# Four stacked conditional layers: the beginning of each scan run, with the copies of du's second half moved and the dt projection placed in two row tiles

## The chip, the cores and the metric

One core of a Trainium2 chip runs the whole program. The metric is the device time of one execution in microseconds; less is better. The engines run beside each other, each through a list of its own: PE is TensorE (matrix products and transposes; PEld is its weight load), ACT is ScalarE, DVE is VectorE, POOL is GpSimd, and SP issues the transfers. An engine executes its list in order and stops at a wait until another engine has counted a semaphore up.

## The reference, cut to what matters

Four layers follow each other on x of shape (2, 1024, 256). Layers 0 and 3 are attention-like. Layer 1 holds one selective scan, layer 2 holds two (one forward, one over the flipped sequence), each for both batch entries, so there are six scans over 1024 tokens, 512 channels and 16 states:

```python
xdbl = xm @ W_xp
dtr, Bm, Cm = jnp.split(xdbl, [DTR, DTR + DS], axis=-1)   # 64, 16, 16
dt = jax.nn.softplus(dtr @ W_dt + b_dt)
...
dA = jnp.exp(dt_t[:, :, None] * A)
hst = hst * dA + (dt_t * x_t)[:, :, None] * B_t[:, None, :]
y = jnp.einsum('bds,bs->bd', hst, C_t)
```

dtr has 64 columns, so the projection to dt contracts over 64 rows. "du" below is the product dt * x. All of it is in float32.

## The kernel before, in words

**A run.** One scan is a `Run` (q = 0 to 5). The 1024 tokens are two chunks of 512, taken in the order `r.order`. Channels lie on partitions in four blocks of 128 (`dt` 0 to 3 in the loops). A run has a beginning (`inputs_t`, `inputs_s`, `inputs_v` on PE, ACT, DVE) and a main part (`run_t`, `run_s`, `run_v`, `run_p`, `run_sp`).

**The beginning.** PE projects a chunk of the input to `xd` (`project_xd_t`, 96 rows: 64 for dt, 16 for B, 16 for C). ACT copies it from PSUM to `XD` in SBUF (`copy_xd_s`, L686). PE projects dt from rows 0 to 63 of it in four matmuls, one for each channel block (`project_dt_t`, L650). ACT takes Abs, Exp and Ln of dt (`size`, `decline`, `log`: L695, L699, L703), DVE the part max(dt, 0) (L763), the sum of the two (delta, L769) and du = delta * u (L771), in the buffer `DUD`. PE turns du of the first chunk into token-major form, four transposes into each of four banks (`turn_du_t`, L656), and ACT and DVE copy or scale the banks into SBUF (`copy_du_s` L735, `copy_du_v` L746, `scale_du_s` L731, `scale_du_v` L742). Between these steps the callbacks `more(0)` to `more(3)` do other work: in layer 1 the product of two weight matrices (`fuse_t`, before the first `turn_du_t`), in layer 2 the projections `z` (runs 2 and 4) or `gates` (runs 3 and 5), eight groups of four matmuls, of which three stand before the turn of du and four behind it. In layer 1 `meanwhile` is an addition and statistics on DVE, in run 2 an addition, in run 3 statistics.

**PSUM.** There are eight banks; `take` waits until the last user of the bank has been read (`banks.give`), and `seek` sets which bank comes next. The four dt banks of the second chunk are 3 to 6. The third group of `more(2)` takes bank 3, and the turned du takes 4 to 7, so both wait until DVE's L763 has read dt of the second chunk.

**The main part.** It has 128 units (16 states, 2 chunks, 4 channel blocks): unit i has a decay on ACT (`decay`, L930), an input formed on PE into banks 4 to 7 (`form_u`, four transposes L845 for even steps, four products L839 for odd ones, three units ahead of the scan) and a scan on DVE (L996). Two units make a pair: POOL multiplies it by C (L1015, 64 in a run), PE adds it up into banks 0 to 3 (`add_up`, L864; pair p at unit 2p + 7). ACT also scales du by B for later units (`scale_b` L907, `spread_b` L914) and keeps the last column of each pair of the first half (`keep`, L922), for which POOL waits. The scanned values have five slots, `r.H`; slots 1 to 4 lie on `DUD`. While the first units run, PE turns du of the second chunk into banks 0 to 3, one bank at each of units 0 to 3; ACT and DVE copy two each at units 3 and 4. `add_up` writes into the same banks, so pair 0 waits for these copies (`open_y`).

**SP.** `run_sp` fetches the rows of C for the steps (`c_load`, L800). In runs 1 and 5 SP first waits for the last turn of du's second chunk and then fetches the weights of the next layer (L1121, L1287), with the first row of C behind it in the same queue. Run 3 and run 5 are begun inside the run before them: `begin_two` projects and copies their first `xd` there.

Of the kernel before, what the change touches and what calls it, by code (L numbers as in the profile page):

```python
# [8 lines left out]
ALU = mybir.AluOpType  # L9
# [102 lines left out]
def program(nc, T, out):  # L112
    with ExitStack() as ctx:
# [495 lines left out]
        CAR = small[:, 136:200]  # L609
        XD = area(WK, S)  # L610
        A_B = [area(WK + 512 * j, 512) for j in range(4)]
# [34 lines left out]
        def project_dt_t(e, w, r, c):  # L646
            w.wait_ge(*act.at(("xd", r.q, c)))
            for m in range(4):
                o = take(w, ("dt", r.q, m, c))
                e.matmul(o, r.wdt[0:64, m * 128:(m + 1) * 128], XD[0:64, c * 512:(c + 1) * 512], start=True, stop=True).then_inc(*pe.up(("dt", r.q, m, c)))  # L650

# [32 lines left out]
        def copy_xd_s(e, w, r, c):  # L684
            w.wait_ge(*pe.at(("xd", r.q, c)))
            e.activation(XD[0:96, c * 512:(c + 1) * 512], bank(("xd", r.q, c))[0:96, :], ACT.Copy).then_inc(*act.up(("xd", r.q, c)))  # L686
            banks.give(("xd", r.q, c), act.now())

        def inputs_s(e, w, r, more, begun=False):
# [17 lines left out]
            more(0)  # L707
            e.preload_act_table_set("natural_log_exp_and_others")
            size(0)
            decline(0)  # L710
            copy_xd_s(e, w, r, r.order[1])
            more(1)
            size(1)
            for c in r.order:
                w.wait_ge(*pe.at(("bt", q, c)))
                e.activation(Bt[:, 4 * c:4 * c + 4, :], bank(("bt", q, c)).rearrange("p (j e) -> p j e", j=4)[:, :, 64:80], ACT.Copy).then_inc(*act.up(("bt", q, c)))
                banks.give(("bt", q, c), act.now())
            log(0)
            decline(1)
# [36 lines left out]
        def inputs_v(e, w, r, meanwhile=None, late=None):  # L756
            q = r.q
            for m in range(4):
                e.tensor_scalar(diag[:, m, :], ident[:, :], col(r.dcol, m), None, ALU.mult).then_inc(*dve.up(("diag", q)))
            for c in r.order:  # L760
                for m in range(4):
                    w.wait_ge(*act.at(("abs", q, m, c)))
                    e.tensor_scalar(r.DT[:, m, c * 512:(c + 1) * 512], bank(("dt", q, m, c)), col(r.bdt, m), 0.0, ALU.add, ALU.max).then_inc(*dve.up(("relu", q, c)))  # L763
                    banks.give(("dt", q, m, c), dve.now())
            for p, c in enumerate(r.order):
                o = slice(c * 512, (c + 1) * 512)
                w.wait_ge(*dve.at(("relu", q, c)))
                w.wait_ge(*act.at(("ln", q, p)))
                e.tensor_tensor(r.DT[:, :, o], r.DT[:, :, o], DUD[:, p, :, :], ALU.add).then_inc(*dve.up(("delta", q, p)))  # L769
                w.wait_ge(*dve.at(("delta", q, p)))  # L770
                e.tensor_tensor(DUD[:, p, :, :], r.DT[:, :, o], r.U[:, :, o], ALU.mult).then_inc(*dve.up(("du", q, p)))  # L771
                if meanwhile and p == 0:
                    meanwhile()
            if late:
                late()
            for j in range(4):
                if first_state(r, j)[2]:
                    scale_du_v(e, w, r, j)
            for j in range(4):
                if first_state(r, j)[2]:  # L780
                    copy_du_v(e, w, r, 0, j)
# [39 lines left out]
        def run_t(e, w, r, back=None, early=None):  # L821
# [54 lines left out]
            for i in range(UNITS):  # L876
                k, dt = divmod(i, 4)
                ci, s = r.steps[k]
                if dt % 2 and i >= 7:
                    add_up((i - 7) // 2)  # L880
                form_u(i + 3)
                if i < 4:
                    turn_du_t(e, w, r, 1, i)
                if dt == 3 and 4 <= s < 8:
                    add_skip(ci, s - 4)
# [10 lines left out]
        def run_s(e, w, r, y, more, early=None):  # L896
# [35 lines left out]

            w.wait_ge(*transfer(f"c_store{q}").at(0))
            w.wait_ge(*dve.at("neg_a"))
            for i in range(4):
# [4 lines left out]
            for j in range(4):  # L940
                if not first_state(r, j)[2]:
                    copy_du_s(e, w, r, 0, j)
            more(3)
            w.wait_ge(*act.at(("bt", q, r.order[1])))
            for j in range(4):
                spread_b(1, j)
            first_half(w, r)
            for i in range(UNITS):
# [5 lines left out]
                if i >= 4:  # L954
                    decay(i)
                if i in (3, 4):
                    copy_du_s(e, w, r, 1, i - 1)
                if dt % 2 and i >= 5:
# [13 lines left out]
        def run_v(e, w, r, y, back=None):  # L972
# [7 lines left out]
            for i in range(UNITS):  # L980
                k, dt = divmod(i, 4)
                ci, s = r.steps[k]
                if i == TAKEN_AT:
                    take_y(0)
                if i in (3, 4):
                    copy_du_v(e, w, r, 1, i - 3)
                w.wait_ge(*decayed.at((q, i)))
# [123 lines left out]
        def layer1_sp(e, w):  # L1111
# [7 lines left out]
            store_c_sp(e, w, runs[1])  # L1119
            w.wait_ge(*pe.at(("dut", 1, 1, 3)))  # L1120
            e.dma_start(W2[:, 0:2816], T["w2"][:, 0:2816]).then_inc(*transfer("w2").up(0))  # L1121
# [155 lines left out]
        def layer2_sp(e, w):  # L1277
# [3 lines left out]
            for q in range(2, 6):  # L1281
# [3 lines left out]
                if q == 5:  # L1285
                    w.wait_ge(*pe.at(("dut", 5, 1, 3)))
                    e.dma_start(W2[:, 0:2048], T["w3"]).then_inc(*transfer("w3").up(0))  # L1287
# [27 lines left out]
        def layer2_s(e, w):  # L1315
            for b in range(NB):
                one, two = runs[2 + 2 * b], runs[3 + 2 * b]

                def begin_two():
                    w.wait_ge(*scanned.at((one.q, UNITS - 2)))  # L1320
                    copy_xd_s(e, w, two, two.order[0])
# [649 lines left out]
```

## Time and profile before

| | |
|---|---|
| median of 3 runs | 1978.16 us (1977.44 to 1983.39) |
| the profiled execution's own time | 1980.28 us |
| span of its trace | 1978.5 us |
| granted TensorE clock, mean | 0.975 of full speed |
| busy: PE, DVE, ACT, POOL | 94%, 81%, 72%, 53% |
| POOL's multiplies L1015 | 384, 896.1 us |

The profile gives for each engine the time in which an instruction was in work; the share of the span is an average over stages that have different limits. In the six runs, some 1100 us of the span, four engines work nearly all the time, and what paces a stage has to be read from the rows of the stage. The last instruction of a chain is followed back to what released it; a share in that chain is not yet a bound where two engines are almost equally loaded.

### The profile page before, as it was taken

The page shows a single profiled execution, that of the slowest core. Times are in us where ns is not written, and L with a number is a line of the kernel's source. Part 1 is how long each engine was busy: PE and PEld are TensorE (multiplying, and loading weights), DVE is VectorE, ACT ScalarE, POOL GpSimd, SP SyncE. Part 2 cuts the span into 40 slices and gives each one's busy share as a digit, 9 for nine tenths or more (in the row PEclk, how much of TensorE's full clock was granted, in tenths as well). Part 3 has the DMA queues.
Part 4 walks back from the last instruction along what each step waited for, and adds up shares of the span by engine and source line. Part 5 has one row for each costly group of instructions (what it writes and reads, how often), then busy time and mean ns, then how long its engine had stood idle before and what let it go on. Part 6 is the DMA issues. An engine that isn't in the chain of part 4 may idle for free.

```text
span 1978.5 us, 32672 instructions
## 1 busy us (share of the span) xinstructions
PE 1865.9 (94%) x12312; PEld 1347.3 (68%) x12312; DVE 1605.2 (81%) x2125; ACT 1422.5 (72%) x2651; POOL 1049.9 (53%) x603
## 2 busy tenths in 40 slices
PE   6989899998999999989999999989998999999997
PEld 3664899748997499959995799679974333232323
DVE  5666899667997699889995999779987999999742
ACT  3426899368993799789974999779854277777775
POOL 3021699416994199929980599469953500003000
PEclk9989999998999999999999999989998799999999
DMA  5022211102111112102110111011101111111000
GB/s 198 1 97 84 65 57 57 49 12 73 57 57 49 34 55 60 49 18 60 55 43 2 38 58 57 23 63 57 55 24 28 41 40 37 37 36 37 19 23 22
DMA packets 57548, 95.19 MB, mean 48 GB/s; under 512 B 14951, under 2 KB 23559, under 8 KB 55982
## 3 DMA queue, kind: packets, MB, share of 16 engines
q1 hardware_dynamic: 55854, 88.90, 15.2%
q0 software_dynamic: 1536, 4.20, 0.7%
q8 instruction: 98, 1.61, 0.3%
q14 instruction: 60, 0.49, 0.1%
HBM read 73.55 MB, written 6.91 MB: 41 GB/s over the span
## 4 chain that ended last, share of the span: by engine, by line
PE 72%; POOL 9%; DVE 8%; issue 5%; ACT 4%; DMA 2%; SPq 1%; DVEq 0%; POOLq 0%; ACTq 0%
PE PS L839 12%; PE PS L864 12%; PE PS L256 9%; POOL A L1015 8%; PE PS L845 6%; PE PS L1599 6%; PE PS L1552 6%; PE PS L1759 5%; PE PS L265 3%; DVE A L1565 2%; PE PS L650 2%; PE PS L871 2%; PE PS L441 2%; PE PS L656 1%; PE PS L243 1%
## 5 line engine op out<-in xcount | busy, mean ns | idle before, releaser
L1015 POOL TENSOR_TENSOR A<-A 128x1024 f32<-128x1024 f32 x384 | 896.1, 2395 | 228.7 <-ACT small L922 163.1
L930 ACT ACTIVATE A<-A,negA 128x512 f32<-128x512 f32 x768 | 546.7, 714 | 32.1 <-DVE A L996 24.1
L996 DVE TENSOR_TENSOR_SCAN A<-A,PS 128x512 f32<-128x512 f32 x384 | 436.0, 1200 | 48.5 <-PE PS L845 19.6
L996 DVE TENSOR_TENSOR_SCAN A<-A,small,PS 128x512 f32<-128x512 f32 x384 | 453.6, 1257 | 8.5 <-ACT A L930 5.2
L864 PE MATMUL PS<-ident,A 128*128 128x128 f32 x3072 | 407.1, 276 | 15.2 <-POOL A L1015 11.8
L839 PE MATMUL PS<-A 128*128 128x128 f32 x3072 | 383.6, 276 | 3.6 <-ACT A L914 3.6
L864 PEld LDWEIGHTS PS<-ident,A 128*128 128x128 f32 x3072 | 353.9, 143 | 22.3 <-POOL A L1015 13.4
L839 PEld LDWEIGHTS PS<-A 128*128 128x128 f32 x3072 | 362.6, 192 | 5.8 <-DVE A L996 3.1
L1565 DVE TENSOR_REDUCE A<-PS 128x1 f32<-128x512 f32 x512 | 319.4, 681 | 40.8 <-PE PS L1552 39.4
L1796 ACT ACTIVATE A<-PS 128x512 f32<-128x512 f32 x512 | 267.5, 602 | 102.2 <-PE PS L1759 101.9
L907 ACT ACTIVATE A<-A,small 128x512 f32<-128x512 f32 x320 | 228.3, 713 | 21.5 <-PE PS L845 21.3
L845 PE MATMUL PS<-ident,A 128*128 128x128 f32 x1360 | 192.8, 280 | 20.5 <-ACT A L907 13.8
L1552 PE MATMUL PS<-A 99*128 99x512 bf16 x480 | 188.4, 401 | 13.0 <-DMA A<-scr 7.6
L1759 PE MATMUL PS<-A 102*128 102x512 bf16 x480 | 178.5, 385 | 5.1 <-ACT A L1796 4.9
L256 PE MATMUL PS<-A,W 128*128 128x512 f32 (+1 forms) x416 | 182.7, 594 | 0.5 <-ACT A L250 0.5
L845 PEld LDWEIGHTS PS<-ident,A 128*128 128x128 f32 x1360 | 160.9, 145 | 26.3 <-DVE A L996 20.2
L230 POOL TENSOR_TENSOR RS<-VE,HALF 128x8 f32<-128x8 f32 (+1 forms) x15 | 27.7, 1846 | 274.5 <-DVE VE L225 274.5
L1530 POOL CAST W<-W 128x32 bf16<-128x32 f32 x32 | 6.7, 211 | 291.8 <-DVE W L1523 217.4
L1552 PEld LDWEIGHTS PS<-A 99*128 99x128 bf16 x480 | 47.2, 98 | 167.3 <-DVE A L1565 122.1
L914 ACT ACTIVATE A<-ident,small 128x128 f32<-128x128 f32 x384 | 148.7, 393 | 6.2 <-PE PS L839 6.2
L256 PEld LDWEIGHTS PS<-A,W 128*128 128x128 f32 (+1 forms) x416 | 74.9, 184 | 97.8 <-issue 93.6
L1599 PE MATMUL PS<-A,W 128*32 128x512 f32 x1024 | 135.9, 604 | 0.0
(193 smaller groups left out, 1832.8 us busy)
## 6 DMA issues: line engine op xcount, KB each, us to landing
A<-scrc SPq DMA_DIRECT2D x192, 256.0 KB, 3.2
A<-A SPq DMA_DIRECT2D x360, 32.0 KB
scr<-A SPq DMA_DIRECT2D x4, 1024.0 KB, 4.8
W<-in_wa SPq DMA_DIRECT2D x2, 1536.0 KB, 9.8
X<-in_x SPq DMA_DIRECT2D x4, 512.0 KB, 5.5
scr<-W SPq DMA_DIRECT2D x128, 1.5 KB
out<-X SPq DMA_DIRECT2D x4, 512.0 KB, 3.0
W<-in_w SPq DMA_DIRECT2D x1, 1984.0 KB, 7.5
```

The source lines that it names most:

```text
L256: t = e.matmul(o[0:M, :], wt(k, m), act_in(k), start=k == 0, stop=k == nk - 1)
L839: t = e.matmul(o[:, j * 128:(j + 1) * 128], r.DUT[:, 4 * ci + j, dt * 128:(dt + 1) * 128], DB[k // 2 % 2][:, j, :], start=True, stop=True)
L845: t = e.transpose(o[:, j * 128:(j + 1) * 128], r.G[(2 * k + j) % 6][:, dt * 128:(dt + 1) * 128], ident[:, :])
L864: t = e.matmul(PS[:, j, dt * 128:(dt + 1) * 128], r.H[pair % HS][:, dt % 2, j * 128:(j + 1) * 128], ident[:, :], start=open_y(ci, j), stop ...
L930: e.activation(A_B[i % 4], r.DT[:, dt, ci * 512:(ci + 1) * 512], ACT.Exp, scale=negA[:, r.n, dt * 16 + s:dt * 16 + s + 1]).then_inc(*decay ...
L996: e.tensor_tensor_scan(h, a, u, init, ALU.mult, ALU.add).then_inc(*scanned.up((q, i)))
L1015: e.tensor_tensor(h, h, CB[k % 2].unsqueeze(1).broadcast_to([128, 2, 512]), ALU.mult).then_inc(*weighed.up((q, pair)))
L1552: e.matmul(o, SQ[j][0:99, nt * 128:(nt + 1) * 128], SK3[j][0:99, c * 512:(c + 1) * 512], start=True, stop=True).then_inc(*pe.up(("trial", ...
L1565: e.tensor_reduce(NM[:, k % 2, q:q + 1], bank(("trial", k, nt, c)), AX.X, ALU.max, negate=True).then_inc(*dve.up(("trial", k, nt, c)))
L1599: t = e.matmul(PV[32 * j:32 * j + 32, c, :], V[:, tile * 272 + 17 * h:tile * 272 + 17 * h + 32], PX[mt % 2][j][:, c * 512:(c + 1) * 512], ...
L1759: e.matmul(o, SK3[sl][0:102, mt * 128:(mt + 1) * 128], SQ[sl][0:102, c * 512:(c + 1) * 512], start=True, stop=True).then_inc(*pe.up(("scor ...
L1796: e.activation(PX[mt % 2][j][:, c * 512:(c + 1) * 512], bank(key), ACT.Exp).then_inc(*act.up(("weights", u, mt, j, c)))
```

## The change

The dt projection of channel blocks 1 and 3 reads rows 64 to 127 of the weights (they are stored twice) and of a second copy of xd, `XD2`, which ACT writes after the first; blocks 0 and 2 stay on rows 0 to 63. PE's wait for the projection is now for the second copy. ACT takes the logarithm of the first chunk before it goes on to the second chunk, and DVE does delta and du of the first chunk before the second chunk's L763; `meanwhile` comes ahead of delta. The turns of du's second chunk move from units 0 to 3 to units 1 to 4, ACT's copies of it from units 3 and 4 to 9 and 10, DVE's from 3 and 4 to 5 and 6, with a wait for the last turn ahead of scan 6. On ACT `more(3)` follows `spread_b(1, ...)`. Runs 3 and 5 no longer preload the table set. SP's two waits ahead of the weight loads are for earlier events.

```diff
-        XD = area(WK, S)
+        XD, XD2 = area(WK, S), area(WK + S, S)
...
         def project_dt_t(e, w, r, c):
-            w.wait_ge(*act.at(("xd", r.q, c)))
+            w.wait_ge(*act.at(("xd_twin", r.q, c)))
             for m in range(4):
-                o = take(w, ("dt", r.q, m, c))
-                e.matmul(o, r.wdt[0:64, m * 128:(m + 1) * 128], XD[0:64, c * 512:(c + 1) * 512], start=True, stop=True).then_inc(*pe.up(("dt", r.q, m, c)))
+                o, h, x = take(w, ("dt", r.q, m, c)), slice(m % 2 * 64, m % 2 * 64 + 64), XD2 if m % 2 else XD
+                e.matmul(o, r.wdt[h, m * 128:(m + 1) * 128], x[h, c * 512:(c + 1) * 512], start=True, stop=True).then_inc(*pe.up(("dt", r.q, m, c)))
...
         def copy_xd_s(e, w, r, c):
+            e.activation(XD2[64:128, c * 512:(c + 1) * 512], bank(("xd", r.q, c))[0:64, :], ACT.Copy).then_inc(*act.up(("xd_twin", r.q, c)))
...
-            e.preload_act_table_set("natural_log_exp_and_others")
+            if not begun:
+                e.preload_act_table_set("natural_log_exp_and_others")
             size(0)
             decline(0)
             copy_xd_s(e, w, r, r.order[1])
+            log(0)
             more(1)
             size(1)
...
-            log(0)
             decline(1)
             log(1)
...
-            for c in r.order:
+            for p, c in enumerate(r.order):
+                o = slice(c * 512, (c + 1) * 512)
                 for m in range(4):
                     w.wait_ge(*act.at(("abs", q, m, c)))
...
-            for p, c in enumerate(r.order):
-                o = slice(c * 512, (c + 1) * 512)
+                if meanwhile and p == 0:
+                    meanwhile()
                 w.wait_ge(*dve.at(("relu", q, c)))
                 w.wait_ge(*act.at(("ln", q, p)))
...
-                if meanwhile and p == 0:
-                    meanwhile()
...
-                if i < 4:
-                    turn_du_t(e, w, r, 1, i)
+                if 1 <= i < 5:
+                    turn_du_t(e, w, r, 1, i - 1)
...
+            w.wait_ge(*pe.at(("bt", q, r.order[1])))
...
-            more(3)
             w.wait_ge(*act.at(("bt", q, r.order[1])))
             for j in range(4):
                 spread_b(1, j)
+            more(3)
...
-                if i in (3, 4):
-                    copy_du_s(e, w, r, 1, i - 1)
+                if i in (9, 10):
+                    copy_du_s(e, w, r, 1, i - 7)
...
-                if i in (3, 4):
-                    copy_du_v(e, w, r, 1, i - 3)
+                if i in (5, 6):
+                    copy_du_v(e, w, r, 1, i - 5)
+                if i == 6:
+                    w.wait_ge(*pe.at(("dut", q, 1, 3)))
...
-            w.wait_ge(*pe.at(("dut", 1, 1, 3)))
+            w.wait_ge(*pe.at(("bt", 1, 1)))
             e.dma_start(W2[:, 0:2816], T["w2"][:, 0:2816]).then_inc(*transfer("w2").up(0))
...
-                    w.wait_ge(*pe.at(("dut", 5, 1, 3)))
+                    w.wait_ge(*pe.at(("mx", 1, 1, 1)))
                     e.dma_start(W2[:, 0:2048], T["w3"]).then_inc(*transfer("w3").up(0))
...
                 def begin_two():
-                    w.wait_ge(*scanned.at((one.q, UNITS - 2)))
+                    w.wait_ge(*scanned.at((one.q, UNITS - 1)))
```

## Rows read from the trace of the kernel before

**Rows 1.** The page: the chain that ended last, shares of the span

```profile
PE 72%; POOL 9%; DVE 8%; issue 5%; ACT 4%; DMA 2%; SPq 1%; DVEq 0%; POOLq 0%; ACTq 0%
```

**Rows 2.** Timeline of POOL in runs 1, 2, 5: start, us, instruction, idle before

```profile
461.53 27.93 POOL L1015 TENSOR_TENSOR A<-A 128x1024 f32<-128x1024 f32 x12 [15.17 <-DMA A<-scrc]
...
500.44 21.01 POOL L1015 TENSOR_TENSOR A<-A 128x1024 f32<-128x1024 f32 x9 [1.02 <-DVE A L996]
...
726.91 107.25 POOL L1015 TENSOR_TENSOR A<-A 128x1024 f32<-128x1024 f32 x46 [0.31 <-DVE A L996]
...
1305.66 37.32 POOL L1015 TENSOR_TENSOR A<-A 128x1024 f32<-128x1024 f32 x16 [45.94 <-DMA A<-scrc]
1344.08 16.44 POOL L1015 TENSOR_TENSOR A<-A 128x1024 f32<-128x1024 f32 x7 [1.09 <-DVE A L996]
```

**Rows 3.** Timeline of TensorE at the beginning of run 2

```profile
651.65 3.70 PE L650 MATMUL PS<-A,W 64*128 64x512 f32 x8
...
655.28 0.24 PEld L256 LDWEIGHTS PS<-A,W 128*96 128x96 f32 x2 [0.76 <-issue]
...
660.60 3.70 PE L650 MATMUL PS<-A,W 64*128 64x512 f32 x8
...
672.04 1.94 PE L656 MATMUL PS<-ident,A 128*128 128x128 f32 x16 [1.75 <-DVE A L771]
673.81 7.03 PE L256 MATMUL PS<-A,W 128*128 128x512 f32 x16
...
690.77 1.06 PE L845 MATMUL PS<-ident,A 128*128 128x128 f32 x8 [2.77 <-ACT A L907]
```

**Rows 4.** Timeline of ACT at the beginning of run 2

```profile
653.76 2.42 ACT L695 ACTIVATE A<-PS,COL 128x512 f32<-128x512 f32 x4
656.22 1.91 ACT L699 ACTIVATE A<-A 128x2048 f32<-128x2048 f32 x1
...
682.64 0.70 ACT L907 ACTIVATE A<-A,small 128x512 f32<-128x512 f32 x1
...
685.81 0.60 ACT L735 ACTIVATE A<-PS 128x512 f32<-128x512 f32 x1 [1.56 <-PE PS L656]
...
688.91 0.19 ACT L922 ACTIVATE small<-A 128x2 f32<-128x2 f32 x1
...
691.14 0.19 ACT L922 ACTIVATE small<-A 128x2 f32<-128x2 f32 x1
```

**Rows 5.** Timeline of SP in run 5: the weights of layer 3, then C

```profile
1298.98 0.33 SPq L1287 DMA_DIRECT2D W<-in_w  x1
1299.43 25.25 SPq L800 DMA_DIRECT2D A<-scrc  x6
```

**Rows 6.** Timeline of TensorE in runs 1 and 5: units 8 and 9 are formed

```profile
457.90 1.06 PE L845 MATMUL PS<-ident,A 128*128 128x128 f32 x8 [2.77 <-ACT A L907]
...
1302.61 1.74 PE L845 MATMUL PS<-ident,A 128*128 128x128 f32 x8 [2.77 <-ACT A L907]
```

**Rows 7.** Timeline of DVE at the beginning of run 2

```profile
662.48 3.33 DVE L763 TENSOR_SCALAR A<-PS,COL 128x512 f32<-128x512 f32 x4 [5.27 <-ACT A L695]
667.27 2.29 DVE L769 TENSOR_TENSOR A<-A 128x2048 f32<-128x2048 f32 x1 [1.46 <-ACT A L703]
```

**Rows 8.** Timeline of ACT at the beginning of run 3

```profile
842.22 1.28 ACT L708 ACT_TABLE_LOAD   x1 [0.23 <-DVE A L819]
...
873.49 0.73 ACT L907 ACTIVATE A<-A,small 128x512 f32<-128x512 f32 x1
```

**Rows 9.** Timeline of TensorE in run 0: the turn of du's first chunk

```profile
200.93 3.32 PE L656 MATMUL PS<-ident,A 128*128 128x128 f32 x16
```

**Rows 10.** Stretches of runs 1 and 2: us, PE, PEld, DVE, ACT, POOL busy, PEclk, DMA

```profile
461.00:465.00 4.00, 1.07 (x5) 1.07 (x6) 0.85 (x1) 2.82 (x6) 3.47 (x2) 0.50 0.02 7
465.00:469.00 4.00, 4.00 (x21) 4.00 (x20) 2.16 (x2) 1.36 (x4) 4.00 (x3) 0.50 0.30 69
...
692.00:696.00 4.00, 4.00 (x23) 4.00 (x23) 4.00 (x5) 4.00 (x11) 4.00 (x2) 0.59 0.21 44
```

More of the change, by code:

```diff
@@ L759, in inputs_v @@
                 e.tensor_scalar(diag[:, m, :], ident[:, :], col(r.dcol, m), None, ALU.mult).then_inc(*dve.up(("diag", q)))
-            for c in r.order:
+            for p, c in enumerate(r.order):
+                o = slice(c * 512, (c + 1) * 512)
                 for m in range(4):
                     w.wait_ge(*act.at(("abs", q, m, c)))
-                    e.tensor_scalar(r.DT[:, m, c * 512:(c + 1) * 512], bank(("dt", q, m, c)), col(r.bdt, m), 0.0, ALU.add, ALU.max).then_inc(*dve.up(("relu", q, c)))
+                    e.tensor_scalar(r.DT[:, m, o], bank(("dt", q, m, c)), col(r.bdt, m), 0.0, ALU.add, ALU.max).then_inc(*dve.up(("relu", q, c)))
                     banks.give(("dt", q, m, c), dve.now())
-            for p, c in enumerate(r.order):
-                o = slice(c * 512, (c + 1) * 512)
+                if meanwhile and p == 0:
+                    meanwhile()
                 w.wait_ge(*dve.at(("relu", q, c)))
```

## The prediction

> **What bounds the kernel now.** I read the page, then the timeline of POOL over the runs, then each engine's timeline over the beginnings. The chain gives most of the span to PE and little to POOL [rows 1], but in the runs this says little: in run 2 POOL does its last 46 multiplies in 107.25 us without a gap, 2.33 us each [rows 2]. It had a gap of 0.31 us before them; in runs 1 and 5, whose first multiply waited for the transfer of C, the gap at this place is 1.0 and 1.1 us [rows 2]. So from the 17th pair on POOL paces a run, and its end is the start of that pair plus 48 x 2.33 = 112 us. I call that start G: 500.4, 726.9 and 1344.1 us in runs 1, 2 and 5.
>
> What sets G? In run 2 PE waits 2.77 us for ACT before it forms unit 8 at 690.8, and from there it works through to G, 36.1 us later [rows 2, 3]; POOL's own first multiply needs ACT's `keep` at 688.9 [rows 4]. So where nothing else is late, G is PE's start of unit 8 (P) plus 36.1. In run 5 the first multiply comes at 1305.7 only, because C is behind the weights in SP's queue, issued at 1299.0 and 1299.4 [rows 2, 5]; run 1 has the same pattern (461.5, [rows 2]).
>
> The reader should therefore follow two things for each run: when P comes, and whether C is there.
>
> **SP's two waits.** In run 5 the multiply began 6.2 us after the issue of C [rows 2, 5]. P is 1302.6 [rows 6], so G without the late C would be 1338.8; it was 1344.1, which is 5.3 us. In run 1 P is 457.9 [rows 6], G would be 494.0 and was 500.4: 6.4 us. After the change run 1's weights are issued in the beginning, more than 5 us before u is ready, and run 5's when the last gates are projected, some 12 us earlier than now; C follows half a microsecond later and lands about when ACT keeps the first pair, which is before PE needs pair 0 (below). Gain 5.3 + 6.4 = 11.7 us. Run 0 has such a queue too, behind the second weight load of layer 1, which still waits for ACT's copies in `more(3)`; there C comes some 2 us after ACT is ready, but 1.5 us or more before PE can use the pair. It costs nothing as long as PE is held longer by the copies.
>
> **The beginning of runs 2 and 4.** I lay out run 2 anew, in times of the trace before.
> ACT: Exp of the first chunk ends at 658.1 [rows 4]. A copy of a bank takes 0.60 us, and the next may start after 0.5 [rows 4]; with xd's and its twin's, the twin is done at 659.2. The logarithm, as long as the Exp (1.9), ends at 661.0. It started at 665.3 before.
> DVE: delta and du take 2.3 us each [rows 7]: du is ready at 665.7, before at 671.9. Then come the four L763, some 0.7 us each while they need not wait (3.33 with waits, [rows 7]): 666.4, 667.1, 667.7, 668.4. The addition of 2.3 us fits between the first L763 and the logarithm; in layer 1's run 1 `meanwhile` is near 6 us and ends du 1.5 us later, but PE is busy with the weight product then.
> PE: the dt projection is eight matmuls at 0.43 us [rows 3]. A matmul of float32 is two such instructions on the same rows. In two row tiles the second of one block can run beside the first of the next, while the issue order is kept: five slots instead of eight, 2.2 us, 1.3 us saved. The trace has no two matmuls side by side; the bounds are 0 and the half, 1.8 us. I take 1.3. It ends the first projection at 653.9 and xd of the second chunk at 657.4; ACT is later than both. The second projection runs 659.3 to 661.5, B's turn until 662.2, two groups until 665.7; the third waits for L763 (666.4) and ends at 668.1. Du's four banks follow, 1.8 us, to 669.9. Before it was 673.8, so 3.9 us are won. `more(3)` takes 6.9 us [rows 3]: 676.8, before 680.7.
> ACT again: Abs until 664.1 (2.4 us for four, [rows 4]), B's copies, Exp, logarithm to 668.2; copies of three groups to 670.0; four decays, four copies (0.6 us from one start to the next) and four `spread_b` (half that, they are a quarter as wide) to 675.8; the four copies of `more(3)` end at 678.2. There unit 0 begins on ACT; before at 682.6 [rows 4]: 4.4 us.
>
> **The copies placed later.** ACT's loop needs 2.2 us for two units (`keep` to `keep`, 688.91 to 691.14, [rows 4]: three of 0.6, a `spread_b` of 0.3 and the 0.1 of `keep`). From its begin to P it took 8.1 us before, 1.6 of them waiting for a turn that ACT's copy needed; that wait and the two copies (1.0 us) leave the stretch, and the first `keep` comes at 682, so POOL starts 7 us earlier. But PE's `add_up(0)`, which stands before unit 10 is formed, waits for the copy that is now at unit 10: four units without decays 1.8, six units 6.7, one decay 0.6, two copies 1.0, together 10.1 us: 688.2. PE has formed 8 and 9 (0.9 us) and three of the eight transposes (0.3) by then, so this equals a P of 687.0, against 690.8: **3.8 us** in run 2, and as much in run 4, whose rows repeat it. The move of the copies by itself costs here what it wins; behind the held PE stand DVE's scan 10, which waits for the slot, and POOL, which has five pairs in hand and is starved only later, at G.
>
> Runs 3 and 5: the table load of 1.28 us [rows 8] goes, and it was on the path, since ACT could not start on dt. Exp ends at 846.6, du is ready at 854.2, the L763 end at 857.0, PE's turn of du at 858.6 (before 862.9), the gates at 865.4, ACT's unit 0 at 867.9 against 873.5 [rows 8]: 5.6 us, less 0.7 for the held `add_up` as in run 2, is **4.9** in each.
>
> Runs 0 and 1: du isn't awaited by PE, the weight product is. PE's path is twin copy +0.5, projections -2.6, one wait for ACT's Exp in place of one of 0.7 us: the turn of du starts at 198.7 instead of 200.9 [rows 9], 2.2 us. It ran at half speed (3.32 us for 16, run 2: 1.94, [rows 3, 9]), which may or may not recur; with ACT's copies behind it I take 2.9 us at unit 0, and after the 0.7 **2.2** in run 0, 2.5 in run 1.
>
> Sum: 2.2 + 2.5 + 3.8 + 4.9 + 3.8 + 4.7 (run 5, a little less, C being close) = 21.9, and 11.7 from SP: 33.6 us.
>
> **What the held PE costs in clock.** In run 1, where PE did 0.9 us of work from 457.9 and then waited until about 464 for POOL, the granted clock is 0.50, the lower level of 1.2 GHz, from 461 to 469 [rows 6, 10]: 5 us after PE resumed, half of them lost. In run 2, after 2.77 us of idle, it is 0.59 over the 4 us from 692 [rows 3, 10]: 3.3 us at the lower level, 1.6 lost. The new gap is 3 to 4 us of idle with 0.9 of work in it. I put it between: 1 us more in each run, bounds 0 and 2.5. That is 6 us. Forecast: 33.6 - 6 = 27.6 us off. The profiled execution had 1980.3 (span 1978.5 and 1.8 around it), 2.1 above the median; I take the gain from the median, 1978.2: 1950.6, so **1951**.
>
> The Trainium skill, "TensorE: Matmul & The Clock Gate", section "Part 3: Packing small matmuls", says that matmuls stay in strict order while those on different row groups run together, starting about 4 ns apart. With two instructions a block that is my five slots; no row here shows it.
>
> **The rivals.**
> (a) The clock doesn't fall further: 33.6 us, 1945. For: there is some work in the gap. Chance 0.15.
> (b) The row tiles don't overlap. Then PE, not ACT, paces the beginning: in run 2 the second projection ends at 664.2, `more(3)` at 678.8, gain 1.8; in runs 3 and 5 2.5; in runs 0 and 1 the twin's wait remains, -1.6. Sum 3.6 + 5.0 - 3.2 = 5.4, with SP's 11.7 about 17, less 6 for the clock: 11, 1967. For: rows on one tile show strict order. Chance 0.20.
> (c) Slower: each change between the two row tiles empties the array. Where the shape changes now, the weight load waits 0.76 us instead of 0.24 [rows 3], 0.5 us more. Three changes inside each of 12 projections are 1.6 us on each; with no overlap 3.1 us a run, nearly all on PE's path, some 19 us: 1967 + 19 = 1986. It decides from 0.3 us a change on. Chance 0.06.
> The skill's "TensorEngine Tiling (Array Packing)", section "Key Properties", speaks against (c): a change of mode drains, a change of tile does not. Half-height matmuls were in use before, so the mode is no new one.
> (d) POOL's own start counts, PE catches up: then each run gains what it gains at unit 0 (4.4, 5.6 and 2.9 us, two runs each, 25.8), the 2.6 of wait and copies (15.6) and, in runs 1 and 5, some 5 us of late C each, less 2 in run 0: 49 us, 1929. Against: PE has no gap between P and G. Chance 0.05.
> (e) It doesn't do what it says: the held `add_up` costs another 4 us a run (clock at half for two stretches, ACT late), and only SP's waits pay: within 5 us of before, 1973 to 1978. Chance 0.07.
>
> **How the numbers follow.** Forecast 0.47, the others as given. A difference under 0.3% (5.9 us) can't be told from none. Faster: forecast, (a), (b), (d) and a small part of (e), 0.88; same: most of (e), 0.06; slower: (c), 0.06. The range takes in (a) and (b) with 3 us at either side for the clock: 1940 to 1969; the likeliest case's own range is 1945 to 1956.
>
> **What the profile after would show.** The turn of du in run 2 (L656) starts some 4 us earlier after the previous run's end and follows L763, not du. L650's eight matmuls take 2.2 us; 3.7 is (b), over 5 is (c). Between forming unit 9 and `add_up(0)` PE idles 3 to 4 us on ACT's copy L735. POOL has a gap of 3 to 4 us in its first 16 multiplies or before the 17th; none is (d). In runs 1 and 5 no first multiply waits for a transfer by more than 1 us. No table load in runs 3 and 5. The forecast is wrong if PE's half-speed stretches last over 5 us in every run, or if PE isn't what G hangs on.

## The result and the profile after

The change makes the kernel faster: 1948.39 us (median of 4 runs, 1946.60 to 1949.29) against 1978.96 for the kernel before, run on the same chip (4 runs, 1977.44 to 1983.39). The ratio is 0.984, with a 95% interval of 0.982 to 0.986. The profiled execution took 1949.29 us, its span is 1947.4. The forecast was 1951, its likeliest case's range 1945 to 1956. In the round of the last four experiments one execution of the kernel before took 4806.18 us; it is part of no ratio.

G, POOL's 17th multiply, is where the prediction measures each run. It comes 30.4 us earlier in run 5, which is the whole gain. The page's chain has less of PE and more of ACT than [rows 1]:

```profile
PE 66%; POOL 9%; ACT 9%; DVE 8%; issue 6%; DMA 1%; SPq 1%; DVEq 0%; ACTq 0%; POOLq 0%
```

POOL's timeline of the kernel after, in runs 1, 2 and 5, against [rows 2]. The bracket is the idle time before the instruction and what ended it:

```profile
451.50 4.67 POOL L1019 TENSOR_TENSOR A<-A 128x1024 f32<-128x1024 f32 x2 [18.14 <-ACT small L923]
...
674.84 4.71 POOL L1019 TENSOR_TENSOR A<-A 128x1024 f32<-128x1024 f32 x2 [30.62 <-ACT small L923]
...
682.57 2.37 POOL L1019 TENSOR_TENSOR A<-A 128x1024 f32<-128x1024 f32 x1 [0.45 <-ACT small L923]
685.80 18.70 POOL L1019 TENSOR_TENSOR A<-A 128x1024 f32<-128x1024 f32 x8 [0.86 <-DVE A L1000]
705.44 9.51 POOL L1019 TENSOR_TENSOR A<-A 128x1024 f32<-128x1024 f32 x4 [0.95 <-DVE A L1000]
716.04 7.04 POOL L1019 TENSOR_TENSOR A<-A 128x1024 f32<-128x1024 f32 x3 [1.09 <-DVE A L1000]
...
1273.08 7.08 POOL L1019 TENSOR_TENSOR A<-A 128x1024 f32<-128x1024 f32 x3 [33.37 <-DMA A<-scrc]
```

Run 1's first multiply no longer waits for C. Run 2 begins its multiplies at 674.84, 14.4 us earlier than before (689.24), but needs 41.2 us to reach the 17th at 716.04, where sixteen multiplies without a gap take 37.3 (run 5, [rows 2]). Gaps of 0.22 to 1.09 us, the longer ones ended by DVE's scan, eat the nearly 4 us between.

PE and ACT of the kernel after at the beginning of run 2, against [rows 3, 4]:

```profile
644.59 2.83 PE L650 MATMUL PS<-A,W 64*128 64x512 f32 x8
...
652.67 1.99 PE L650 MATMUL PS<-A,W 64*128 64x512 f32 x8
...
661.46 1.91 PE L656 MATMUL PS<-ident,A 128*128 128x128 f32 x16
```

```profile
641.26 0.59 ACT L686 ACTIVATE A<-PS 96x512 f32<-96x512 f32 x1 [2.74 <-issue]
...
670.86 0.71 ACT L908 ACTIVATE A<-A,small 128x512 f32<-128x512 f32 x1
...
674.51 0.19 ACT L923 ACTIVATE small<-A 128x2 f32<-128x2 f32 x1
...
678.97 0.57 ACT L737 ACTIVATE A<-PS 128x512 f32<-128x512 f32 x1
...
680.53 0.58 ACT L737 ACTIVATE A<-PS 128x512 f32<-128x512 f32 x1
```

From ACT's first copy of xd to unit 0 (L908, L907 before) it is 29.6 us, before 34.3 (648.33 to 682.64). The eight dt matmuls take 1.99 us, not 3.70, in ten of the twelve projections; in the first of runs 2 and 4 they take 2.83, at full clock, and no run here says why. ACT's `L737` (L735 before) is the copy that `add_up(0)` waits for; asked who waits for it, the trace of after answers for all runs:

```profile
  PE PS L865: 13.1, 11
```

13.1 us in 11 waits, some 2 a run; before, no `add_up` waited for it.

**The clock.** For each kernel one row of windows for the beginning of each run, 44 us each, PE's granted clock behind the last engine. Before:

```profile
196.00:240.00 44.00, 38.77 (x309) 37.24 (x308) 36.22 (x32) 38.71 (x85) 24.38 (x11) 0.92 0.19 61
436.00:480.00 44.00, 35.00 (x242) 33.70 (x241) 35.05 (x44) 33.29 (x71) 22.12 (x9) 0.77 0.19 63
672.00:716.00 44.00, 41.19 (x310) 37.06 (x311) 41.88 (x37) 40.37 (x88) 26.76 (x12) 0.96 0.15 43
870.00:914.00 44.00, 39.86 (x342) 39.44 (x343) 40.10 (x38) 41.83 (x93) 33.89 (x15) 0.96 0.13 38
1100.00:1144.00 44.00, 41.23 (x346) 39.88 (x345) 38.62 (x36) 40.68 (x90) 33.60 (x15) 0.96 0.14 37
1292.00:1336.00 44.00, 35.94 (x294) 35.17 (x293) 34.95 (x32) 37.51 (x84) 30.34 (x14) 0.88 0.23 72
```

After:

```profile
196.00:240.00 44.00, 38.64 (x298) 36.77 (x297) 34.23 (x31) 38.10 (x83) 25.67 (x11) 0.88 0.21 66
436.00:480.00 44.00, 38.50 (x301) 37.04 (x301) 35.78 (x33) 38.12 (x83) 26.58 (x12) 0.88 0.13 40
664.00:708.00 44.00, 42.09 (x319) 37.71 (x318) 39.99 (x37) 41.67 (x92) 30.68 (x14) 0.96 0.12 37
852.00:896.00 44.00, 40.59 (x320) 38.06 (x319) 37.24 (x36) 39.54 (x87) 31.96 (x14) 0.92 0.11 37
1078.00:1122.00 44.00, 42.08 (x338) 38.02 (x337) 40.38 (x39) 42.60 (x95) 32.88 (x15) 1.00 0.12 37
1268.00:1312.00 44.00, 40.61 (x348) 39.50 (x347) 39.73 (x37) 40.64 (x89) 36.98 (x16) 0.96 0.22 77
```

A clock of 1.00 is the level of 2.4 GHz, and 44 us times what is missing from it is what the lower level of 1.2 GHz took away: 24.2 us in the six windows before, 17.6 after. The windows don't begin at the same place of every run; taken from each run's first xd copy to its G it is 23.9 and 17.1 us. The clock was lost less, not more.

### The profile page after: what moved, and what is told of

Read it like the earlier page. It is cut to its first block, busy times and chain, and to the rows that moved or that the text cites. A ratio compares the mean times of both kernels' runs of the same rounds, so it can differ in the third digit from the quotient of the medians.

```text
span 1947.4 us, 32682 instructions
## 1 busy us (share of the span) xinstructions
PE 1845.8 (95%) x12312; PEld 1335.2 (69%) x12312; DVE 1602.8 (82%) x2125; ACT 1424.0 (73%) x2661; POOL 1049.0 (54%) x603
## 4 chain that ended last, share of the span: by engine, by line
PE 66%; POOL 9%; ACT 9%; DVE 8%; issue 6%; DMA 1%; SPq 1%; DVEq 0%; ACTq 0%; POOLq 0%
PE PS L865 12%; PE PS L840 11%; POOL A L1019 8%; PE PS L256 7%; PE PS L1603 6%; PE PS L1556 6%; PE PS L846 5%; PE PS L1763 5%; PE PS L265 3%; DVE A L1569 2%; PE PS L872 2%; ACT A L931 2%; PE PS L441 2%; ACT A L908 1%; DVE ST L206 1%
## 5 line engine op out<-in xcount | busy, mean ns | idle before, releaser
L931 ACT ACTIVATE A<-A,negA 128x512 f32<-128x512 f32 x768 | 546.7, 714 | 30.8 <-DVE A L1000 24.1
L865 PE MATMUL PS<-ident,A 128*128 128x128 f32 x3072 | 409.1, 276 | 21.5 <-ACT A L737 13.1
L865 PEld LDWEIGHTS PS<-ident,A 128*128 128x128 f32 x3072 | 352.9, 143 | 31.2 <-ACT A L737 15.6
L908 ACT ACTIVATE A<-A,small 128x512 f32<-128x512 f32 x320 | 228.3, 714 | 21.7 <-PE PS L846 21.3
L256 PE MATMUL PS<-A,W 128*128 128x512 f32 (+1 forms) x416 | 184.9, 598 | 3.3 <-DVE A L766 2.9
L846 PEld LDWEIGHTS PS<-ident,A 128*128 128x128 f32 x1360 | 158.7, 143 | 11.9 <-issue 4.6
L256 PEld LDWEIGHTS PS<-A,W 128*128 128x128 f32 (+1 forms) x416 | 75.1, 185 | 102.7 <-issue 91.5
```

Source lines behind the costliest of these rows:

```text
L256: t = e.matmul(o[0:M, :], wt(k, m), act_in(k), start=k == 0, stop=k == nk - 1)
L846: t = e.transpose(o[:, j * 128:(j + 1) * 128], r.G[(2 * k + j) % 6][:, dt * 128:(dt + 1) * 128], ident[:, :])
L865: t = e.matmul(PS[:, j, dt * 128:(dt + 1) * 128], r.H[pair % HS][:, dt % 2, j * 128:(j + 1) * 128], ident[:, :], start=open_y(ci, j), stop ...
L931: e.activation(A_B[i % 4], r.DT[:, dt, ci * 512:(ci + 1) * 512], ACT.Exp, scale=negA[:, r.n, dt * 16 + s:dt * 16 + s + 1]).then_inc(*decay ...
```

## The experiments

Each kernel is compared with before, run between its own rounds; the medians of before lay between 1978.5 and 1979.9. The table stands ahead of the runs because every reading uses it: by how much each run gets shorter against before, worked out from POOL's timelines (G of a run less G of the run before it; run 0 from the span's start).

| kernel | time, us | ratio, 95% interval | run 0 | 1 | 2 | 3 | 4 | 5 | clock lost, us |
|---|---|---|---|---|---|---|---|---|---|
| after | 1948.4 | 0.982 to 0.986 | -1.0 | 8.0 | 3.8 | 4.0 | 5.2 | 10.3 | 17.1 |
| e1_one_tile | 1970.7 | 0.994 to 0.997 | -7.7 | 1.3 | 3.9 | 2.6 | 2.0 | 7.9 | 22.2 |
| e2_copies_old | 1945.7 | 0.982 to 0.985 | 1.5 | 11.9 | 3.7 | 6.3 | 1.8 | 11.5 | 11.9 |
| e3_copies_7_8 | 1933.2 | 0.977 to 0.979 | 1.6 | 13.3 | 6.5 | 7.8 | 5.0 | 13.0 | 3.4 |
| e4_sp_old | 1963.0 | 0.990 to 0.993 | -2.2 | 1.8 | 3.8 | 3.9 | 3.8 | 5.1 | 29.0 |
| e5_sp_only | 1967.6 | 0.993 to 0.996 | -2.4 | 8.4 | 0.0 | 0.4 | 0.1 | 5.4 | 11.9 |
| e6_order_old | 1964.0 | 0.991 to 0.994 | -2.9 | 8.5 | 0.4 | 0.4 | 0.3 | 5.9 | 30.7 |
| e7_preload | 1951.9 | 0.985 to 0.988 | -0.5 | 8.4 | 3.8 | 3.5 | 5.3 | 8.7 | 17.1 |
| e8_c_first | 1932.3 | 0.975 to 0.977 | 0.9 | 11.0 | 6.5 | 7.8 | 6.4 | 13.1 | 10.2 |
| e9_turns_0_3 | 1936.2 | 0.976 to 0.979 | 0.8 | 10.9 | 6.5 | 7.7 | 4.9 | 13.0 | 10.2 |
| e10_tiles_only | 1974.7 | 0.997 to 0.999 | 0.7 | 2.4 | 0.3 | 2.0 | -1.5 | 2.5 | 22.2 |
| e11_order_only | 1970.9 | 0.994 to 0.997 | -2.3 | 3.6 | 2.5 | 2.1 | 1.8 | 2.1 | 18.8 |
| e12_tiles_order | 1964.1 | 0.991 to 0.993 | -1.8 | 3.8 | 3.6 | 3.2 | 3.8 | 3.4 | 22.2 |

Run 0's column has a share of work that no kernel changes: its first xd copy comes between 177.28 us (before) and 181.00 us (e6_order_old) in these traces. A difference under 3.7 us in that column says nothing.

The last column is what the lower level of the clock took away in the profiled execution between each run's first xd copy and its G, the six runs added up; before lost 23.9. It moves with the times: e4_sp_old and e6_order_old, 14.6 and 15.6 us slower than after, lose 11.9 and 13.6 us more than it, and e5_sp_only, 10.9 faster than before, loses 12.0 less. So the price of a part, as it is taken below, is that of its waits and of the clock that goes with them, and no run separates the two. Executions of one kernel differ in the same way: of e4_sp_old the fastest took 1955.82 us at a granted clock of 0.976 over the whole span, the slowest 1964.65 at 0.970.

**One row tile.** In the kernel after:

```diff
-                o, h, x = take(w, ("dt", r.q, m, c)), slice(m % 2 * 64, m % 2 * 64 + 64), XD2 if m % 2 else XD
+                o, h, x = take(w, ("dt", r.q, m, c)), slice(0, 64), XD
```

> The changed kernel with the four matmuls of a dt projection all on rows 0 to 63 again; the second copy of xd is still made and waited for. Theory: without the overlap each projection takes 3.7 us in place of 1.9, PE and no longer ACT paces the beginnings, and the sum of the prediction falls from 33.6 to about 17: some 16 us slower than the changed kernel, about 1965. Rival, the projection is hidden behind ACT's work in all runs: within 3 us of 1948.

1970.7 us, 22.3 slower than after, where 16 were expected: the tiles do overlap, and the rival that ACT hides it falls. By the table 13.4 of the 20.3 us between the two lie in runs 0 and 1. PE in run 0 of e1_one_tile:

```profile
180.04 4.69 PE L650 MATMUL PS<-A,W 64*128 64x512 f32 x8 [1.35 <-ACT A L687]
184.66 6.03 PE L256 MATMUL PS<-A,W 128*96 128x512 f32 x8
191.98 3.70 PE L650 MATMUL PS<-A,W 64*128 64x512 f32 x8 [1.29 <-ACT A L687]
```

and the windows of it that hold this stretch:

```profile
180.00:184.00 4.00, 3.96 (x8) 1.56 (x8) 1.73 (x3) 3.34 (x4) 0.00 (x0) 0.83 0.00 0
184.00:188.00 4.00, 4.00 (x5) 1.24 (x5) 1.28 (x2) 2.60 (x2) 0.00 (x0) 0.50 0.00 0
```

The same stretch of after:

```profile
179.95 1.99 PE L650 MATMUL PS<-A,W 64*128 64x512 f32 x8 [1.36 <-ACT A L687]
181.86 3.67 PE L256 MATMUL PS<-A,W 128*96 128x512 f32 x8
...
186.83 1.99 PE L650 MATMUL PS<-A,W 64*128 64x512 f32 x8 [1.30 <-ACT A L687]
```

So the tiles save 1.7 us on each projection where the clock is whole (3.70 against 1.99), and with one tile and the twin's wait of 1.35 us the clock falls to its lower level: 4.69 in place of 3.70, and L256, which is the same work in both, 6.03 in place of 3.67. The two add up to 6.8 us in run 0, half of it clock, and run 1 repeats it. In runs 2 to 5, where ACT and DVE set the beginning, the tiles bring 0 to 3 us each. The twin copy and its wait stay in this kernel, so 22.3 us is what the overlap brings against a kernel that pays for the twin and doesn't use it; no run takes both out of the kernel after.

**Du's copies and turns where they were.** In the kernel after, ACT's and DVE's copies at units 3 and 4 and the turns at units 0 to 3 again.

```diff
-                if 1 <= i < 5:
-                    turn_du_t(e, w, r, 1, i - 1)
+                if i < 4:
+                    turn_du_t(e, w, r, 1, i)
...
-                if i in (9, 10):
-                    copy_du_s(e, w, r, 1, i - 7)
+                if i in (3, 4):
+                    copy_du_s(e, w, r, 1, i - 1)
...
-                if i in (5, 6):
-                    copy_du_v(e, w, r, 1, i - 5)
+                if i in (3, 4):
+                    copy_du_v(e, w, r, 1, i - 3)
```

> The changed kernel with the turns and copies of du's second half at their old units (turns at 0 to 3, all copies at 3 and 4). Theory of the prediction: the later copies hold add_up(0) and cost about what they win, a little more with the clock; from unit 0 on ACT to the 17th multiply it should be about 44.3 us again (45.2 to 46.1 in the changed kernel), less so in runs 2 and 4, where ACT would wait longer for the turn: some 5 us faster than the changed kernel, about 1943. Rival, the placement is what brings the gain: 6 us or more slower, 1954 or above.

1945.7 us, 2.7 faster than after; the intervals overlap. The theory had 5 faster, and the rival of 1954 or above falls. The later copies, which stand in the title, bring nothing that can be measured, and may cost a little. The reason is in run 2 of e2_copies_old, ACT's rows, then POOL's:

```profile
664.48 0.72 ACT L908 ACTIVATE A<-A,small 128x512 f32<-128x512 f32 x1
...
668.74 0.60 ACT L737 ACTIVATE A<-PS 128x512 f32<-128x512 f32 x1 [2.63 <-PE PS L656]
...
671.84 0.20 ACT L923 ACTIVATE small<-A 128x2 f32<-128x2 f32 x1
```

```profile
672.18 37.35 POOL L1019 TENSOR_TENSOR A<-A 128x1024 f32<-128x1024 f32 x16 [34.36 <-ACT small L923]
```

ACT waits 2.63 us for a turn, so POOL's first multiply, behind `keep`, comes 7.7 us after unit 0 instead of 4.0; but then POOL has sixteen multiplies without a gap. The kernel after starts POOL early and starves it by nearly 4 us: from unit 0 to the 17th multiply run 2 takes 45.3 us here and 45.2 there, the same time spent in another place. In runs 0, 1, 3 and 5, where ACT waits less for the turn, it takes 43.4 to 43.7 us here.

**ACT's copies at units 7 and 8.** In the kernel after:

```diff
-                if i in (9, 10):
-                    copy_du_s(e, w, r, 1, i - 7)
+                if i in (7, 8):
+                    copy_du_s(e, w, r, 1, i - 5)
```

> The changed kernel with ACT's two copies at units 7 and 8 in place of 9 and 10: the turn they wait for is done by then. Theory: PE's add_up(0) starts 2.2 us earlier, PE's gap ahead of it shrinks, and as the 17th multiply hangs on PE, each run gains about 2 us: 12 us, about 1936. Rival, the 17th multiply hangs on something else (POOL's own start, DVE): no change, 1948.

1933.2 us (1931.9 to 1938.4), 15 faster than after, where 12 were expected, and 2.2% faster than before. POOL in runs 1 and 2 of e3_copies_7_8:

```profile
447.52 2.37 POOL L1019 TENSOR_TENSOR A<-A 128x1024 f32<-128x1024 f32 x1 [16.80 <-ACT small L923]
450.22 2.36 POOL L1019 TENSOR_TENSOR A<-A 128x1024 f32<-128x1024 f32 x1 [0.34 <-ACT small L923]
...
672.26 32.67 POOL L1019 TENSOR_TENSOR A<-A 128x1024 f32<-128x1024 f32 x14 [0.32 <-DVE A L1000]
705.46 18.69 POOL L1019 TENSOR_TENSOR A<-A 128x1024 f32<-128x1024 f32 x8 [0.54 <-DVE A L1000]
```

Four microseconds from unit 0 to the first multiply, 38.6 us from there to the 17th: both halves of the stretch are short. PE's waits for L737 in `add_up` are 3.0 us in all against 13.1, and the clock stays whole, as in run 1:

```profile
436.00:480.00 44.00, 39.68 (x350) 38.26 (x350) 39.66 (x37) 42.84 (x96) 31.82 (x14) 1.00 0.13 37
```

In the same six places its windows lack 3.5 us of clock, all in run 0, where after lacks 17.6. This is its fastest execution: the two kernels below with copies as early as this lost 10.2 us in theirs.

**SP's old waits, and the new ones alone.** The first in the kernel after, the second in the kernel before with the signs turned round:

```diff
-            w.wait_ge(*pe.at(("bt", 1, 1)))
+            w.wait_ge(*pe.at(("dut", 1, 1, 3)))
...
-                    w.wait_ge(*pe.at(("mx", 1, 1, 1)))
+                    w.wait_ge(*pe.at(("dut", 5, 1, 3)))
```

> The changed kernel with SP's two old waits ahead of the weight loads in runs 1 and 5. Theory: the first row of C comes late again and costs 6.4 and 5.3 us: about 11 to 12 us slower than the changed kernel, 1960; the first multiply of runs 1 and 5 waits for the transfer. Rival, as the 17th multiply is now held by add_up anyway, the late C hides behind it: under 5 us.

> The kernel before with only SyncE's two new waits (the weight loads of runs 1 and 5). Theory: 5.3 us in run 5 and 6.4 in run 1 come out of the span, since both runs' POOL multiplies began late for want of C: 1967 us (ratio 0.994); and if the 14.6 us that the opposite run showed hold here as well, 1964. Where the two numbers differ, the reason would be that with the new first part the wait costs more. Rival: the time freed is eaten by du's copies, which here still stand at units 3 and 4 and pace the beginning in those runs too: 1975 to 1979.

1963.0 and 1967.6 us: 14.6 slower than after, 10.9 faster than before. With the old waits the first multiplies of runs 1 and 5 stand behind C again:

```profile
462.13 9.29 POOL L1019 TENSOR_TENSOR A<-A 128x1024 f32<-128x1024 f32 x4 [27.55 <-DMA A<-scrc]
...
1290.02 30.30 POOL L1019 TENSOR_TENSOR A<-A 128x1024 f32<-128x1024 f32 x13 [41.33 <-DMA A<-scrc]
```

By the table it is 6.2 + 5.2 = 11.4 us in runs 1 and 5 in the one and 8.4 + 5.4 = 13.8 in the other. The rest of each total lies in runs that the edit doesn't touch. In the kernel before it came within 1 us of the forecast; in the kernel after it costs 3 us more than was expected, in an execution that lost 11.9 us more clock. That this part pays without the others is shown, and the rivals (that du's copies eat it, that the late C hides) fall; that it adds whole to any of them is not.

**The order of the first chunk's log, delta and du undone.** In the kernel after (the same on DVE: delta and du behind both chunks' L766, `meanwhile` behind the first du):

```diff
             copy_xd_s(e, w, r, r.order[1])
-            log(0)
             more(1)
...
+            log(0)
             decline(1)
             log(1)
```

> The kernel after, with the two reorderings of the first chunk undone: ACT takes the first chunk's logarithm behind the B copies again, and DVE computes delta and du of the first chunk after both chunks' relu. Theory: the first du is late and unit 0's multiplies, the turns and add_up(0) move with it: 2 to 3 us in each of six runs, 12 to 18 us in all: 1960 to 1966 us. Rival: the second chunk is what paces, so that the order within the first part matters little: 1948 to 1952.

1964.0 us, 15.6 slower, within the theory's 12 to 18, but 3.4 to 4.9 us in each of runs 2 to 5 and nothing in run 1 (8.5 against 8.0), where 2 to 3 in each of six were expected. The lower clock is part of it: 1.7 to 3.4 us more in each of these four runs. PE in run 2 of e6_order_old waits for du again, and ACT's first decays wait for DVE's addition, which now stands between the two du:

```profile
664.53 2.41 PE L656 MATMUL PS<-ident,A 128*128 128x128 f32 x16 [2.49 <-DVE A L774]
```

```profile
666.62 2.56 ACT L933 ACTIVATE A<-A,negA 128x512 f32<-128x512 f32 x4 [1.48 <-DVE X L1351]
```

**C ahead of the second weights in run 0; turns earlier.** In e3_copies_7_8 the second weight load of layer 1 is issued behind the first two rows of C. e9_turns_0_3 has this too, with the turns back at units 0 to 3 and ACT's copies at 6 and 7:

```diff
                 ci, s = r.steps[k]
+                if k == 2 and third:
+                    third()
```

> The kernel with ScalarE's copies at units 7 and 8 (1933.2 us), and in run 0 SyncE issues the second part of the z and c weights behind the first two rows of C in place of ahead of them. Theory: POOL's first multiply of run 0, which waited for C until 213.98, starts up to 3 us earlier, and run 0's end with it, since POOL has no gap from there on: 1930 to 1932 us. Rival: C is limited by its own store, not by the weights in the queue, or the weights then come late for the next projection: 1933 to 1936.

> As the one before (C first in run 0), and du's turns at units 0 to 3 again with ScalarE's two copies at units 6 and 7. Theory: with turns one unit earlier, add_up(0) and what follows come no later and POOL, which has almost no gap left before its 17th multiply, gains nothing: within 2 us of the kernel above. Rival: the turns still compete with the first add_up, which pays 1 us a run: 5 us under or over it.

1932.3 and 1936.2 us. Neither can be told from 1933.2 (the intervals overlap). The second is 3.9 us above the first, more than the theory's 2, and their intervals overlap as well. C is issued at 195.0 us instead of 208.5 and POOL's first multiply is then released by ACT:

```profile
195.00 0.80 SPq L803 DMA_DIRECT2D A<-scrc  x2
...
214.34 2.38 POOL L1021 TENSOR_TENSOR A<-A 128x1024 f32<-128x1024 f32 x1 [48.87 <-ACT small L925]
```

From unit 0 (210.35) that is 4.0 us, where in e3_copies_7_8 it was 6.0 (207.99 to 213.98, ended by C). But all of run 0 is later in this trace, from its first xd copy on (180.16 against 178.51), so the 2.0 us are gone in G. That the move is worth 2 us is argued from this stretch and not shown by the times.

**The parts alone in the kernel before.** The row tiles with their twin copy; the order; and both.

> The kernel before with the row tiles alone (the twin copy, and the wait for the last scan in front of it in runs 3 and 5); everything else as before. So far, taking single parts out of the kernel after cost 22 us (tiles), 15.6 (order) and 14.6 (SyncE's waits), together far more than the 30 that the change brings. Theory: PE's projections and the late first du stand beside each other in the chain, and the one left in place holds unit 0: the tiles without the order bring 3 to 6 us, 1972 to 1976. Rival: the parts simply add, and the copies at units 3 and 4 are what costs: the tiles alone bring 15 to 20, 1958 to 1963.

> The kernel before with the order alone: ScalarE's first logarithm right behind the second xd copy, and DVE's delta and du of the first chunk ahead of the second chunk's relu, with the work in between moved ahead of them. Theory: with one row tile PE's projections hold the second chunk back, and the earlier first du waits for them all the same: 1975 to 1981, no change to speak of. Rival: the order pays by itself, as the 15.6 us of its removal say: 1962 to 1968.

> Both of the above in the kernel before. Theory: together they bring what neither brings alone, about 17 to 20 us, 1958 to 1962; with SyncE's two waits (11 us where they were alone) and the copies' 0 this makes the change's 30. Rival: a sum of the two runs above, whatever they are.

Against before in their own rounds the ratios are 0.998, 0.995 and 0.992, that is 4.4, 9.1 and 16.0 us. The tiles confirm the theory; the order alone, at 1970.9, lies between the theory and its rival. Both together come to 1964.1, 2 us outside the theory's 1958 to 1962. That is 2.5 us more than the sum of the two, which is within the intervals, so the rival that the parts simply add isn't refuted. In run 2 the effect can be seen, from the first xd copy to unit 0: 34.3 us before, 34.2 with the tiles, 32.4 with the order, 30.8 with both. With the tiles alone PE is early and stands before the turn of du, which is late as ever:

```profile
667.03 3.00 PE L656 MATMUL PS<-ident,A 128*128 128x128 f32 x16 [2.50 <-DVE A L772]
```

**The table load kept in runs 3 and 5.** In the kernel after:

```diff
-            if not begun:
+            if True:
                 e.preload_act_table_set("natural_log_exp_and_others")
```

> The kernel after with the load of the logarithm's table set issued in runs 3 and 5 as well. Theory: 1.3 us of ScalarE between the copy and the first exponential is on the way to unit 0, twice: 2 to 3 us slower than after, 1950 to 1952. Rival: ScalarE waits for the projections there anyway: no difference, 1947 to 1949.

1951.9 us (1950.9 to 1955.1), above every run of after: 3.6 us slower by the medians, but the intervals overlap. Unit 0 comes 30.0 and 30.1 us behind the first xd copy in runs 3 and 5 against 28.7 and 28.8, so the load is on the way to it, as the theory has it; by the table 0.5 and 1.6 us of that reach G, and the rest of the 3.6 isn't located.

**The sum.** Tiles and order 16.0 and SP 10.9, both in the kernel before, and the table load 3.6 in the kernel after: 30.5 us, and the copies nothing. The change brings 30.6. The match is closer than the parts are known: each has an interval of some 2.5 us to either side, SP is 14.6 when it is taken out of the kernel after, and e2_copies_old, all of the change but the copies and turns, brings 32.8 by its median. `more(3)` behind `spread_b(1, ...)` was not tested by itself.

## Why the prediction was right

**G as the end of each run** held: G moved by 30.4 us, the time by 30.6. By runs, with the clock's 1 us taken off each: 1.2, 7.9, 2.8, 3.9, 2.8, 9.0 were forecast, and -1.0, 8.0, 3.8, 4.0, 5.2, 10.3 came. Run 0 is short in part because its first xd copy, which no part of the change touches, came 1.4 us later in this execution; runs 4 and 5 bring 2.4 and 1.3 us more than forecast.

**SP's two waits**: 11.7 forecast, 11.4 and 13.8 in the two experiments by the table, 14.6 and 10.9 by the medians. Run 5's first multiply is still released by C, which SP issues behind the weights, 6.1 us ahead of it; but it starts 4.2 us behind unit 0 (1268.89), where run 2 needs 4.0:

```profile
1266.58 0.33 SPq L1291 DMA_DIRECT2D W<-in_w  x1
1267.02 21.72 SPq L801 DMA_DIRECT2D A<-scrc  x5
```

**The beginning.** Unit 0 was to come 4.4 us earlier in run 2 and 5.6 in run 3, and came 4.7 and 5.6 earlier (from the first xd copy; run 3: 828.34 to 857.05 against 839.22 to 873.49). In run 0 it was 2.2 for 2.9.

**The row tiles** were sized too small: 2.2 us forecast for eight matmuls from a count of slots, 1.99 measured, little over the half of 3.70. Eight slots of 0.43 are 3.44, so one projection ends 0.26 us behind its slots; with that, five slots would be 2.4 and four are 1.98. The Trainium skill's rule in "TensorE: Matmul & The Clock Gate", "Part 3: Packing small matmuls", that matmuls on different row groups run together, agrees with it; the five slots were my own reading of its strict order, and they fall. So does (c): eight matmuls with their tile changes in 1.99 us leave no room for 0.3 us a change, as "TensorEngine Tiling (Array Packing)", "Key Properties", of the same skill has it. Rival (b)'s price was about right: 1967 forecast without the overlap, 1970.7 run.

**The held add_up**: the second copy was to be done 10.1 us behind unit 0 and was, within 0.2 (680.53 and 0.58, unit 0 at 670.86). "The move of the copies by itself costs here what it wins" is what e2_copies_old shows. PE's idle time on these copies is some 2 us a run, where 3 to 4 were to be seen: in run 2 it comes to `add_up(0)` only 7.85 us behind unit 0 (678.71), and three of its eight instructions run before the last of its two waits, of 0.47 and 1.24 us.

**The clock** is the term that was wrong in sign. I took 6 us off for it; the windows have 6.6 us less of loss after than before, made up of 4.8 in run 1 and 3.5 in run 5, whose long wait for C is gone, 1.8 in run 4, and 1.8 more lost in each of runs 0 and 3. This clock gain is part of what SP's waits and the shorter beginnings measure; without a deduction the sum of 33.6 was 3 us too high. The deduction had no ground in what came, and the forecast of 27.6 is as far below 30.6 as 33.6 is above it: that 1951 lay 3 us from the result, and not further, is partly luck.

**PE as the only pace of G** was too narrow. Before, run 2's first multiply starts at 689.24 and the 17th at 726.91, 37.7 us, where sixteen without a gap take 37.3:

```profile
689.24 37.35 POOL L1015 TENSOR_TENSOR A<-A 128x1024 f32<-128x1024 f32 x16 [37.97 <-ACT small L922]
```

POOL's own start held G as much as PE did, both to within 0.4 us. I read the gap of 0.31 us as PE's doing alone. In e2_copies_old all six runs need 37.6 or 37.7 us from the first to the 17th, so there G hangs on POOL's start; for that kernel the prediction's own sign of being wrong, "if PE isn't what G hangs on", would be met. In the kernel after it isn't: POOL takes 41.2 us in run 2 and waits for what feeds it, as the prediction had it, and rival (d), given 0.05 at 1929, lies 19 us from the result. Its mechanism, POOL's early start with PE keeping up, is what a move of the copies by two units brings out, at 1933; that this lies near its number is no test of it, as it is another kernel.

## What to carry to other kernels

When a queue of work is released at its head and fed from behind, look at both the start of the first item and the time from there to the one that begins the steady stretch; a move that only exchanges one for the other brings nothing, and the place between (here units 7 and 8) can bring both. Parts that shorten parallel arms of one beginning can be worth more together than alone (unit 0 of run 2: 0.1 and 1.9 us, together 3.5), so test them in pairs before one is dropped; in the whole time, 4.4 and 9.1 against 16.0 us, the intervals here don't show it. What a late transfer costs is read at the start of the steady stretch and not at the item that waits for it: in run 1, measured from the first xd copy, SP's earlier issue brings the first multiply 6.7 us and the 17th 8.4 us forward in the kernel before, and the old waits put them 9.4 and 6.3 us back in the kernel after.

## What the runs showed that I had not expected

- Eight float32 matmuls of 64 rows by 512 columns in two alternating row tiles take 1.99 us against 3.70 on one.
- A wait of 1.35 us ahead of a one-tile projection came with a fall of PE's clock to the lower level (windows 0.83, then 0.50); the same wait of 1.36 us ahead of the two-tile projection did not, and neither did 0.74 us ahead of a one-tile projection in the kernel before. It turned a saving of 3.4 us in run 0 into 6.8. Why it falls in the one and not the other isn't settled.
- The lower level cost 24.2 us of the beginnings before, 17.6 after and 3.5 with the copies at units 7 and 8: the last step, 15 us by the medians, gives back 14.1 us of clock in its profiled execution and closes most of POOL's gaps. How the 15 us divide between the two wasn't separated, and the clock varies: e8_c_first, with the same copies, lost 6.8 us more between the first xd copies and G and took 1936.1 us in the execution that was profiled.
